# Two 16-wide attentions on one Trainium2 core: the split of the row maxima, the division and the split of the keys are rearranged

## What is computed

```python
# L0 (L3 the same without biases; its values are its keys, its heads are laid out d-major)
q = split_heads(query @ w_q.T + b_q)
k = split_heads(key @ w_k.T + b_k)
v = split_heads(value @ w_v.T + b_v)
scores = jnp.einsum('bhqd,bhkd->bhqk', q, k) / scale
attn = jax.nn.softmax(scores, axis=-1)
ctx = jnp.einsum('bhqk,bhkd->bhqd', attn, v)
out = ctx.transpose(0, 2, 1, 3).reshape(B, -1, D_MODEL) @ w_o.T + b_o
```

## Time and profile before

| | |
|---|---|
| profiled execution | 3109.23 us, span 3107.4 us |
| median of 3 runs | 3110.44 us |
| TensorE busy | 2591.0 us, 83% |
| VectorE / ScalarE / GpSimd busy | 1834.2 / 1322.3 / 912.3 us |
| `score_T` of L0x, first to last | 89.1 to 433.8 us of the span |
| `score` of L3x, steady rounds | some 2091 to 2335 us |

### The profile page before, as it was taken

How to read it: one execution, slowest core, us unless ns; L and a number is a source line. 1 busy time by engine, 2 the same in 40 slices (tenths; PEclk the granted TensorE clock), 3 DMA queues, 4 the chain that set the end, 5 groups by cost and what they waited for, 6 DMA issues and landing times. The chain is left out here.

```text
span 3107.4 us, 51343 instructions
## 1 busy us (share of the span) xinstructions
PE 2591.0 (83%) x19362; PEld 1809.9 (58%) x19362; DVE 1834.2 (59%) x3996; ACT 1322.3 (43%) x2630; POOL 912.3 (29%) x755
## 2 busy tenths in 40 slices
PE   2899967879686999999999847479998429999998
PEld 1566634657573555555555425346664418888887
DVE  5788867837645666666666548868886412222222
ACT  1566558815552443434444348536665101111111
POOL 1566640002200211111111202336665352222222
PEclk8999988989898999999999979889999559999999
DMA  5666610010002000000000000087672522332232
GB/s 142 135 134 124 129 52 1 1 62 1 6 1 67 8 5 8 5 8 5 8 6 3 1 31 1 23 150 137 127 137 41 159 78 34 99 72 67 66 72 32
DMA packets 154904, 173.90 MB, mean 56 GB/s; under 512 B 24352, under 2 KB 134208, under 8 KB 154688
## 3 DMA queue, kind: packets, MB, share of 16 engines
q1 hardware_dynamic: 129408, 136.72, 20.2%
q0 software_dynamic: 14496, 20.36, 3.5%
q10 hardware_dynamic: 10784, 13.90, 1.4%
HBM read 120.70 MB, written 49.71 MB: 55 GB/s over the span
## 5 line engine op out<-in xcount | busy, mean ns | idle before, releaser
L268 POOL TENSOR_TENSOR L2x_halves_sum<-L2x_probs 128x512 f32<-128x512 f32 x128 | 162.9, 1273 | 809.1 <-ACT L2x_probs L282 809.1
L1365 PE MATMUL L3f_pH<-L3f_xgT,L3f_W 128*128 128x256 f32 x1184 | 265.7, 382 | 8.9 <-ACT L3f_hT L1394 8.2
L1373 PE MATMUL L3f_pY<-L3f_W,L3f_hT 128*128 128x256 f32 x1184 | 261.7, 379 | 0.0
L365 DVE TENSOR_REDUCE L2x_mx<-L2x_pS 128x2 f32<-128x512 f32 x256 | 165.1, 687 | 163.1 <-PE L2x_pS L495 163.0
L1365 PEld LDWEIGHTS L3f_pH<-L3f_xgT,L3f_W 128*128 128x128 f32 x1184 | 226.1, 191 | 42.7 <-ACT L3f_hT L1394 10.6
L1394 ACT ACTIVATE L3f_hT<-L3f_pH,L3f_b 128x256 f32<-128x256 f32 x148 | 69.5, 474 | 411.5 <-PE L3f_pH L1365 346.8
L1373 PEld LDWEIGHTS L3f_pY<-L3f_W,L3f_hT 128*128 128x128 f32 x1184 | 222.1, 190 | 28.7
L2583 POOL TENSOR_TENSOR L3x_halves<-L3x_probs 128x512 f32<-128x512 f32 x128 | 166.0, 1298 | 136.3 <-ACT L3x_probs L2624 136.1
L2583 POOL TENSOR_TENSOR L0x_halves<-L0x_probs 128x512 f32<-128x512 f32 x128 | 165.4, 1292 | 125.4 <-ACT L0x_probs L2624 125.2
L2772 DVE TENSOR_REDUCE L0x_mx<-L0x_pS 128x2 f32<-128x512 f32 x256 | 163.9, 684 | 58.6 <-PE L0x_pS L2898 58.4
L2772 DVE TENSOR_REDUCE L3x_mx<-L3x_pS 128x2 f32<-128x512 f32 x256 | 162.8, 682 | 54.6 <-PE L3x_pS L2898 54.4
(11 more groups left out here) (584 smaller groups left out, 6073.2 us busy)
## 6 DMA issues: line engine op xcount, KB each, us to landing
L0x_k_stack<-L0x_k_parts_dram SPq DMA_DIRECT2D x112, 128.0 KB, 7.3
L3x_k_stack<-L3x_k_parts_dram SPq DMA_DIRECT2D x112, 128.0 KB, 7.8
L0x_q_stack<-L0x_q_parts_dram SPq DMA_DIRECT2D x32, 384.0 KB, 5.8
L3x_q_stack<-L3x_q_parts_dram SPq DMA_DIRECT2D x32, 384.0 KB, 6.0
L3f_W<-in_L3f_W ACTq DMA_DIRECT2D x12, 1024.0 KB
L3f_xg<-tokens_by_expert SPq DMA_DIRECT2D x38, 260.0 KB
L0x_q_parts_dram<-L0x_q_parts SPq DMA_DIRECT2D x16, 384.0 KB, 2.8
L0x_k_parts_dram<-L0x_k_parts SPq DMA_DIRECT2D x16, 384.0 KB, 3.1
```

What stands on the lines that cost most here:

```text
L268: nc.gpsimd.tensor_tensor(halves_sum[n % 2][:, :, :], probs[n % 2][:, :, 0, :], probs[n % 2][:, :, 1, :], ALU.add).then_inc(halved, 1)
L365: nc.vector.tensor_reduce(mx[:, :, 2 * p + u], pS[u][:, :].rearrange("p (j s) -> p j s", j=TB), AX.X, ALU.max).then_inc(max_done, 1)
L1365: ins = nc.tensor.matmul(pH[c % 4][:, 0:TILE], W1[par][:, kc, c * P:(c + 1) * P], xgT[:, kc, :], start=kc == 0, stop=kc == KC - 1)
L1373: ins = nc.tensor.matmul(pY[j][:, 0:D], hT[:, c, j * P:(j + 1) * P], W2[par][:, c, :], start=c == 0, stop=c == HCH - 1)
```

## The change

- **Order.** Scores and maxima of a batch lie one step earlier (from t = 4 instead of t = 5). "mT" is filled at t = 4 behind "out".
- **Maxima.** `split_max` is gone. The maxima are kept in f32 (`mx`, two buffers, 128 columns wide), transposed in f32, and split from PSUM: ScalarE writes the negated high part (t = 4), VectorE (`low_max`, t = 5) the low part and frees the bank. `send_rows` stays at t = 6.
- **Keys.** `rest_k` goes ahead of the maxima of t = 4, `mid_k` to ScalarE, `low_k` right behind the maxima of t = 4.
- **Division.** The product of the Newton step is written back to PSUM instead of to `ln_sum`.

```diff
-    FILLS = {0: "q", 1: "xnT", 2: "k", 4: "out", 5: "mT", 6: "v"}
+    FILLS = {0: ("q",), 1: ("xnT",), 2: ("k",), 4: ("out", "mT"), 6: ("v",)}
...
-        b, pair = (r + 2, t - 5) if t >= 5 else (r + 1, t + 3)
+        b, pair = (r + 2, t - 4) if t >= 4 else (r + 1, t + 4)
...
-        mx = sb("mx", [P, TB, H])
-        nm = sb("nm", [P, TB, P], BF16)
-        mT = [sb(f"mT{i}", [2 * H, S], BF16) for i in range(2)]
+        mx = [sb(f"mx{i}", [P, TB, P]) for i in range(2)]
+        m_parts = [[sb(f"m_{n}{i}", [H, S], BF16) for i in range(2)] for n in ("hi", "lo")]
...  (ScalarE)
+            def mid_k(b):
+                bank, n = place["k", b]
+                act.wait_ge(free[bank], n + 1)
+                nc.scalar.activation(k_parts[:, :, 1, :], k_rest[:, :, :], ACT.Copy).then_inc(k_mid, 1)
...  (take_mT)
-                nc.scalar.activation(mT[b % 2][:, :], src[0:2 * H, 0:S], ACT.Copy).then_inc(taken, 1)
+                nc.scalar.activation(m_parts[0][b % 2][:, :], src[0:H, 0:S], ACT.Copy, scale=-1.0).then_inc(m_hi, 1)
...
-                    if t == 5 and 0 <= r + 1 < B:
+                    if t == 4 and 0 <= r + 3 < B:
+                        mid_k(r + 3)
+                    if t == 4 and 0 <= r + 1 < B:
                         take_mT(r + 1)
...  (VectorE)
-            def split_max(b):
...
+            def low_max(b):
+
+                bank, _ = place["mT", b]
                 dve.wait_ge(m_hi, b + 1)
+                nc.vector.scalar_tensor_tensor(m_parts[1][b % 2][:, :], pM[bank][0:H, 0:S], -1.0, m_parts[0][b % 2][:, :],
+                                               ALU.mult, ALU.subtract).then_inc(free[bank], 1)
...  (divide)
-                nc.vector.tensor_tensor(t, pO[g][:, S:2 * S], r, ALU.mult).then_inc(newton_1, 1)
+                nc.vector.tensor_tensor(total, total, r, ALU.mult).then_inc(newton_1, 1)
                 dve.wait_ge(newton_1, n + 1)
-                nc.vector.scalar_tensor_tensor(t, t, 2.0, r, ALU.subtract, ALU.mult).then_inc(newton_2, 1)
+                nc.vector.scalar_tensor_tensor(t, total, 2.0, r, ALU.subtract, ALU.mult).then_inc(newton_2, 1)
...
+                    if t == 4 and 0 <= r + 3 < B:
+                        rest_k(r + 3)
                     for b, i in scores_at(r, t):
                         maximum(b, i)
+                    if t == 4 and 0 <= r + 3 < B:
+                        low_k(r + 3)
...
-                    if t == 4 and 0 <= r + 1 < B:
-                        split_max(r + 1)
-                    if t == 4 and 0 <= r + 3 < B:
-                        rest_k(r + 3)
-                        mid_k(r + 3)
+                    if t == 5 and 0 <= r + 1 < B:
+                        low_max(r + 1)
                     if t == 5 and 0 <= r - 1 < B:
                         residual(r - 1)
-                    if t == 5 and 0 <= r + 3 < B:
-                        low_k(r + 3)
...  (TensorE, fill "mT")
-                    pe.wait_ge(m_lo, b + 1)
+                    pe.wait_ge(max_done, H * (b + 1))
                     for j in range(TB):
-                        ins = nc.tensor.matmul(dst[:, j * P:(j + 1) * P], nm[:, j, :], core.ident_b[:, :],
-                                               start=True, stop=True)
+                        ins = nc.tensor.transpose(dst[:, j * P:(j + 1) * P], mx[b % 2][:, j, :], core.ident[:, :])
```

More of the change, by code:

```diff
@@ L2397, in head_of @@
         return 8 * g + 2 * (i % E4) + i // E4
-    FILLS = {0: "q", 1: "xnT", 2: "k", 4: "out", 5: "mT", 6: "v"}
+    FILLS = {0: ("q",), 1: ("xnT",), 2: ("k",), 4: ("out", "mT"), 6: ("v",)}
     AHEAD = {"q": 3, "xnT": 4, "k": 3, "out": -1, "mT": 1, "v": 1}
     def fills_of(r, t):
-        named = [(FILLS[t], r + AHEAD[FILLS[t]])] if t in FILLS else []
+        named = [(name, r + AHEAD[name]) for name in FILLS.get(t, ())]
         return [(name, b) for name, b in named if 0 <= b < B]
     def scores_at(r, t):
-        b, pair = (r + 2, t - 5) if t >= 5 else (r + 1, t + 3)
+        b, pair = (r + 2, t - 4) if t >= 4 else (r + 1, t + 4)
         return [(b, 2 * pair + e) for e in range(2)] if 0 <= b < B else []
@@ L2468, in narrow_attention @@
         full, free = ([sem(f"{n}{i}") for i in range(2)] for n in ("full", "free"))
-        k_hi, k_rest_ready, k_mid, k_split = (sem(n) for n in ("k_hi", "k_rest_ready", "k_mid", "k_split"))
+        k_hi, k_mid, k_split = (sem(n) for n in ("k_hi", "k_mid", "k_split"))
         q_rest_ready, q_mid, q_split = (sem(n) for n in ("q_rest_ready", "q_mid", "q_split"))
         k_saved, q_saved = sem("k_saved"), sem("q_saved")
-        s_ready, max_done, m_hi, m_lo = (sem(n) for n in ("s_ready", "max_done", "m_hi", "m_lo"))
+        s_ready, max_done, m_hi = (sem(n) for n in ("s_ready", "max_done", "m_hi"))
         t_ready, p_ready, pv_done = sem("t_ready"), sem("p_ready"), sem("pv_done")
@@ L2661, in take_k @@
                 ins.then_inc(k_hi, 1)
+            def mid_k(b):
+                bank, n = place["k", b]
+                act.wait_ge(free[bank], n + 1)
+                nc.scalar.activation(k_parts[:, :, 1, :], k_rest[:, :, :], ACT.Copy).then_inc(k_mid, 1)
             def take_mT(b):
-                src, taken = filled(act, "mT", b)
+                src, _ = filled(act, "mT", b)
                 if b >= 2:
                     act.wait_ge(rows_in[b % 2], 32 * (b // 2))
-                nc.scalar.activation(mT[b % 2][:, :], src[0:2 * H, 0:S], ACT.Copy).then_inc(taken, 1)
+                nc.scalar.activation(m_parts[0][b % 2][:, :], src[0:H, 0:S], ACT.Copy, scale=-1.0).then_inc(m_hi, 1)
             def send_rows(b):
@@ L2674, in send_rows @@
                     act.dma_start(q_stack[b % STACKS][TERM_ROWS + i:TERM_ROWS + i + 1, :, :],
-                                  mT[b % 2][i * H:(i + 1) * H, :]).then_inc(rows_in[b % 2], 16)
+                                  m_parts[i][b % 2][:, :]).then_inc(rows_in[b % 2], 16)
             def inverse(b, g):
@@ L2715, in _ @@
                 nc.vector.memset(v[i][:, :, :, :], 0.0)
-            nc.vector.memset(nm[:, :, :], 0.0)
+            for i in range(2):
+                nc.vector.memset(mx[i][:, :, :], 0.0)
             nc.vector.memset(ones[:, :], 1.0).then_inc(cleared, 1)
@@ L2737, in rest_k @@
                 ins.then_inc(taken, 1)
[L2739 to L2742, removed]
             def low_k(b):
@@ L2768, in maximum @@
                 n = H * b + i
-                if i == 0 and b:
-                    dve.wait_ge(m_lo, b)
+                if i == 0 and b == 0:
+                    dve.wait_ge(cleared, 1)
+                if i == 0 and b >= 2:
+                    bank, m = place["mT", b - 2]
+                    dve.wait_ge(full[bank], m + 1)
                 dve.wait_ge(s_ready, n + 1)
-                nc.vector.tensor_reduce(mx[:, :, head_of(i)], pS[n % 2][:, :].rearrange("p (j s) -> p j s", j=TB),
+                nc.vector.tensor_reduce(mx[b % 2][:, :, head_of(i)], pS[n % 2][:, :].rearrange("p (j s) -> p j s", j=TB),
                                         AX.X, ALU.max).then_inc(max_done, 1)
-            def split_max(b):
[L2777 to L2781, removed]
+            def low_max(b):
+                bank, _ = place["mT", b]
                 dve.wait_ge(m_hi, b + 1)
-                nc.vector.scalar_tensor_tensor(nm[:, :, H:2 * H], mx[:, :, :], -1.0, nm[:, :, 0:H],
-                                               ALU.mult, ALU.subtract).then_inc(m_lo, 1)
+                nc.vector.scalar_tensor_tensor(m_parts[1][b % 2][:, :], pM[bank][0:H, 0:S], -1.0, m_parts[0][b % 2][:, :],
+                                               ALU.mult, ALU.subtract).then_inc(free[bank], 1)
             def divide(b, g):
@@ L2789, in divide @@
                 dve.wait_ge(inv_ready, n + 1)
-                r, t = inv[g][:, :], ln_sum[g][:, :]
-                nc.vector.tensor_tensor(t, pO[g][:, S:2 * S], r, ALU.mult).then_inc(newton_1, 1)
+                r, t, total = inv[g][:, :], ln_sum[g][:, :], pO[g][:, S:2 * S]
+                nc.vector.tensor_tensor(total, total, r, ALU.mult).then_inc(newton_1, 1)
                 dve.wait_ge(newton_1, n + 1)
-                nc.vector.scalar_tensor_tensor(t, t, 2.0, r, ALU.subtract, ALU.mult).then_inc(newton_2, 1)
+                nc.vector.scalar_tensor_tensor(t, total, 2.0, r, ALU.subtract, ALU.mult).then_inc(newton_2, 1)
                 dve.wait_ge(newton_2, n + 1)
```

## The result

| | before | after |
|---|---|---|
| median of 6 runs, us | 3110.12 (3108.25 to 3120.74) | 3099.36 (3092.99 to 3106.47) |
| ratio, 95% | | 0.996 [0.9941, 0.998] |
| profiled execution, us | 3109.23 | 3103.20 |

What follows compares the result with a forecast made beforehand. The prediction held that VectorE's order at steps 3 to 5 sets a round's end through TensorE's waits, with DMA close behind. Gains of 25.0 us (L0x) and 12.3 (L3x) made 37.3, giving 3073 us; 8-in-10 range 3052 to 3095.

Steps and rivals of the forecast that it cites:

- rival E: Division: the PSUM write costs its 0.43 us back, 3077 us; chance 0.50 together with the main forecast.
- TensorE's path: TensorE's own time per round once its waits go: 20.78 us in the first attention (L0x), 19.67 in the last (L3x).
- The stacks: Chain from query save to last stack landing limits rounds: 21.0 us in L3x; in L0x 20.4, under TensorE's 20.78.
- The lock: VectorE's `low_k` and GpSimd's `low_q` at t = 4 block each other: 0.3 us on the query save, between 0 and 0.9.
- The rows of the maxima: Row DMAs sent at t = 6 land 1.1 us late in L3x, hidden by the stacks' cost, 0 in L0x.
- rival D: Late rows of the maxima bind, 1 us more per L0x round: 3084 us; 0.20 together with another rival.
- Ends: Filling and draining rounds: first rows about 2.5 us later, yet a net gain of 4 us in L0x, 0.5 in L3x.
- the sum: Total gain over both attentions: L0x 25.0 us and L3x 12.3 us with their ends, together 37.3 us.

Runs made afterwards that it cites:

- x4: The whole change, but from the fifth batch of an attention each stack load moves an eighth of its bytes (scores on old data): 3042.91 us, 0.982 of before.
- v1: z3 with GpSimd's `low_q` ahead of the `halve` of t = 4, so the query save goes out sooner: 3048.17 us, 0.9834 of before.
- x3: The whole change with `low_max` ahead of the maxima of t = 5 and the row DMAs issued at t = 5: 3071.96 us, 0.9913 of before.
- z2: x2 with `low_k` at t = 6 instead of t = 5, so the key save and loads start later: 3086.59 us, 0.9911 of before.
- x2: x1 plus `rest_k` ahead of the maxima of t = 4 and `mid_k` on ScalarE; maxima as before: 3105.17 us, 1.0022 of before.
- v2: The whole change with `low_q` ahead of the `halve` of t = 4, rows still sent at t = 6: 3188.39 us, 1.0279 of before.
- z1: The whole change with `low_max` and the row DMAs a step earlier for the first batch alone: 3095.36 us, 0.9943 of before.
- v3: The whole change without the division's edit: 3100.2 us, 0.9999 of before.
- z0: The whole change measured again, beside the kernel before on the experiments' chip: 3102.69 us, 0.9963 of before.
- x1: The kernel before with the division's edit alone: 3088.15 us, 0.9961 of before.
- z3: x3 with the first batch's "mT" filled ahead of that step's scores and its `low_max` ahead of the maxima: 3078.7 us, 0.9902 of before.

## Why the prediction was wrong

**Right, by its own steps.** "mT" starts without a wait for `rest_k`. The division: 0.85 to 0.42 us, and the product written to PSUM takes 0.42, so nothing (rival E fell). `mid_k` on ScalarE: 0.63 us for 0.60. *TensorE's path*: 20.87 and 19.60 to 19.73 us in x4 and v1, for 20.78 and 19.67. L0x rounds: 20.87 for 20.95; the eleven rounds gained 20.8 us (251.0 less 230.2) for 21.0. *The stacks*: L3x rounds without a wait for rows took 20.1 to 21.6 us for 21.0, with `k_stack` waited for in front of the first score of t = 4, 0.5 to 1.8 us. And v1, with no load made smaller, shows that an earlier start of the chain, `low_q`, is enough to bring L3x to 19.64 us. What the forecast left out here is that such a wait can cost more than its length: behind the one of 1.80 us the clock fell.

**The lock** was priced at 0.3 us on the query save, out of 0 to 0.9: `low_q` takes 1.61 us for the 1.15 that it always took before, so 0.46 us; `low_k` 1.34 for 0.68 in L3x. The forecast quoted the Trainium skill (SBUF — State Buffer, "SBUF: two separate sides"): the ports that VectorE and GpSimd share are a lock, which a VectorE instruction with two SBUF inputs takes too, and whoever holds it blocks the other for a whole instruction. The trace agrees: at 2157.14 `low_k` starts during a `halve` that ends at 2157.93 and ends 0.55 us behind it, and `low_q` then ends 1.02 us behind `low_k`.

**The step that failed is *The rows of the maxima*.** It sized the landing at 3.4 us from one row (a `score_T` let go 3.4 us after the second issue), put 1.1 us at most on a round of L3x and none on L0x, and rival D took 1 us a round. In the steady rounds of before, 1.8 and 1.9 us were the rule, and after the landings run from 1.8 to 9.1: not a duration with some scatter, but one that depends on what moves when the DMA is issued. Rounds of seven kernels, by the time from the first load's issue to the first row DMA's:

| kernel, round | rows against loads, us | landed after, us |
|---|---|---|
| x3, L0x | -3.50 | 2.2, 3.0 |
| z2, L0x | -3.03 | 1.8, 1.9 |
| v1, L0x | -1.87 | 3.4, 3.2 |
| before, L0x | -1.56 | 1.8, 1.9 |
| after, L0x | -1.22 | 2.7, 2.5 |
| x2, L0x | -0.94 | 3.1, 5.5 |
| v2, L3x | +0.37 | 6.2, 7.0 |
| after, L3x | +0.46 | 6.0, 6.9 |
| after, start of L0x | +1.07 | 6.6, 8.2 |

Behind the first load the rows took 6 us and more. Ahead of it they took 1.8 to 5.5 us, and not by the order of these two queues alone: in after, x2, x3 and v1 a save is under way or starts with them, and what each transfer adds wasn't tried. The forecast wrote of the rows, the save and the loads "Now they always lie beside these", and still took the landing from a kernel in which none was above 3.4 us. It didn't ask which of the two queues would issue first, although it also expected the key save directly behind the query save, which is what brings the loads up to the rows. By its own numbers (query save at 4.58 us of t = 4 with the lock, loads some 3.4 us later, rows 1.0 us into t = 6, at 6.27) the rows of a steady round go out 1.7 us ahead of the loads; 1.2 us was measured, and those rounds came out as forecast. The starts it didn't work out at all, and in five rounds (one each in after, z1 and v3, two in z0) the slow "out" behind a wait for `k_stack` used the 1.2 us up.

**And so *Ends* failed.** It had a gain of 4.5 us, from a delay of some 2.5 us at the start, part of it hidden. The first batch's rows were issued 4.1 and 3.2 us later than before, counted from the start of L0x and of L3x; that took them behind the loads, and the second of them took 5.0 and 5.7 us longer from issue to landing. By the two profiles 17.5 us were lost there (some 13.5 against x1). In the terms of the sum: ends -17.5 for +4.5, the rest of L3x 7.1 for 11.8 (the round of 27.26 us lost 6), L0x 21.3 for 21.0, which makes 10.9 for 37.3. The draining rounds are in the last two numbers. Putting the rows right (x3) gives 27.4 us; that a start without its 1.2 and 3.5 us would give 32 is an estimate, and z3, which has the 3.5 us back but not the 1.2, can't be told from x3.

**The forecast's own signs** didn't cover this. It would call itself wrong if L0x rounds were above 21.5 us or a new wait on VectorE appeared; of the eleven L0x rounds one was, at 21.66 us, the mean was 20.93, and no such wait appeared. The sign that did come was the one it gave for D, a wait of `score_T` for the rows, but at the starts and in single rounds instead of in each.

**Open.** The layers between take 5.9 us more in the profile of after; other kernels' profiles have 1554 to 1560 us there, with or without the change, so I don't put it down to it. Why z3, with no loss left in the fill of L3x, isn't faster than x3 isn't settled. Nor is it settled when a wait for the stacks is followed by the fall of the clock: in steady rounds it was behind waits of 1.73 to 2.12 us, and not behind others of up to 2.26 us (v3, at 2313.07). And the order isn't all: the round of 23.58 us in z0 has its rows 1.21 us ahead of the loads, like its neighbours, and they landed in 4.6 and 6.3 us instead of 2.7 and 2.4.

## What to carry to other kernels

A small DMA on which the next step hangs is priced by what will be in flight when it is issued, not by its landing so far: write down, for the order after the change, which queue issues first. Where work is taken off an engine that gates a bulk transfer, the transfer moves forward, and a critical small one beside it must be moved ahead of it; each place where they pass is worth an experiment that moves only the small one. Ask also what a short wait of TensorE does to the clock behind it, and which transfer the slower matmuls delay. Take the first batch as a case of its own, since its order isn't that of the steady rounds.

## What the hardware showed

- In the change, two DMAs of 8 KB, issued from another queue 0.5 to 1.1 us after the first of ten that move 2 MB, land in 6.0 to 9.1 us instead of the 1.8 and 1.9 of most rounds before. The packets show where the time goes. In the round of 2162.93, their queue (q10) moved nothing in the first 2 us, 8 packets from 2165 to 2167, and most of the rest here:

```profile
q1 hardware_dynamic: 69, 0.20, 102.6%
q10 hardware_dynamic: 34, 0.01, 6.8%
```

(2167 to 2168 us: packets, MB, share of the 16 engines; q1 is SyncE's). The Trainium skill says (DMA: Bandwidth & Descriptors, "Issuing engines are not separate DMA queues") that DMAs of different engines run on the same 16 and interleave. From 2167 on the trace agrees; the first 2 us, in which one queue alone moved, no run here explains.
- Waits of TensorE of 4.5 to 7.8 us are followed by a stretch at a lower granted clock (0.55 and 0.62 over the stretches above), so they cost more than their length. v2 waits 97.1 us for rows in its two attentions, v1 0.9, and v2 takes 140 us more: some 1.5 times.
- Shorter waits can do it too. Behind waits for `k_stack` of 1.73 to 2.12 us, six steady rounds (one each in after, z1, v3 and x3, two in z0) have their "out" in 2.90 to 3.58 us; in all other steady rounds of the thirteen profiles it takes 1.89 to 1.97. Before, "mT" waited 0.91 us in a steady round, and the granted clock over ten of them was 1.00.
